# Attention step: scores and minimum of a group's fourth head before the transposes of P's first head, and the output products dealt 5 and 7

## The reference

```python
q = rope(rmsnorm(x @ Wq)); k = rope(rmsnorm(x @ Wk)); v = x @ Wv      # 32 q heads, 8 kv heads of 128
k_all = concatenate([k_cache[block_table], k]); v_all likewise        # 512 cached keys + 128 new
scores = where(valid, q @ k_all.T * SCALE, -1e30)
probs = softmax(scores)                                               # called P here
x = x + (probs @ v_all) @ Wo
```

## Time and profile before

| what | value |
|---|---|
| median of 3 runs | 1405.84 us (1405.07 to 1408.55) |
| the profiled execution | 1408.16 us, its span 1406.0 us |
| busy: TensorE, weight loads | 1392.1 us (99%), 1206.8 us (86%) |
| busy: VectorE, ScalarE, GpSimd | 1094.7 us (78%), 852.8 us (61%), 802.5 us (57%) |
| granted clock of TensorE, mean | 0.998 |

### The profile page before, as it was taken

How to read it: one execution, slowest core, us unless ns; L and a number is a source line. 1 busy time by engine, 2 the same in 40 slices (tenths; PEclk the granted TensorE clock), 3 DMA queues, 4 the chain that set the end, 5 groups by cost and what they waited for, 6 DMA issues and landing times.

```text
span 1406.0 us, 26951 instructions
## 1 busy us (share of the span) xinstructions
PE 1392.1 (99%) x8035; PEld 1206.8 (86%) x8035; DVE 1094.7 (78%) x2220; ACT 852.8 (61%) x2092; POOL 802.5 (57%) x799
## 2 busy tenths in 40 slices
PE   7999999999999999999999999999999999999999
PEld 5888888888888888888888888888888888888887
DVE  7788888888888888888888888888888666654543
ACT  6677666666666666666666666666677423433332
POOL 6555555555555666666666666666566331444442
PEclk9999999999999999999999999999999999999999
DMA  5533333333333222322222223232332540343341
GB/s 179 164 110 110 111 103 104 107 107 104 104 102 105 69 71 65 72 65 65 66 73 67 66 66 74 65 69 49 85 91 65 155 105 24 105 140 106 113 124 69
DMA packets 191440, 129.87 MB, mean 92 GB/s; under 512 B 118832, under 2 KB 158384, under 8 KB 188864
## 3 DMA queue, kind: packets, MB, share of 16 engines
q1 hardware_dynamic: 181808, 110.98, 29.7%
q10 hardware_dynamic: 9072, 16.07, 3.8%
q0 software_dynamic: 416, 1.11, 0.3%
HBM read 125.25 MB, written 24.64 MB: 107 GB/s over the span
## 4 chain that ended last, share of the span: by engine, by line
PE 96%; DMA 1%; DVE 1%; SPq 1%; POOL 1%; issue 0%; ACT 0%; DVEq 0%
PE banks L328 22%; PE banks L329 22%; PE banks L330 22%; PE banks L1456 12%; PE banks L1430 10%; PE banks L1392 2%; PE banks L1400 1%; PE banks L1687 1%; PE banks L1701 1%; PE banks L1514 1%; DMA acc<-in_x 1%; PE banks L1640 1%; PE banks L1408 0%; DMA kv_raw<-in_kv,row_at 0%; SPq L348 0%; PE banks L1539 0%
## 5 line engine op out<-in xcount | busy, mean ns | idle before, releaser
L754 ACT ACTIVATE prob<-prob,nbias 128x640 f32<-128x640 f32 x256 | 210.3, 822 | 145.7 <-DVE nbias L1037 145.7
L1008 DVE TENSOR_TENSOR pt_pair<-banks,pt_pair 128x640 fp32r<-128x640 f32 x256 | 210.8, 824 | 100.8 <-ACT pt_pair L750 98.3
L1037 DVE CUSTOM_DVE_ANT_0 prob<-banks,mask,q_rs 128x640 f32<-128x640 f32 x256 | 220.1, 878 | 39.5 <-PE banks L330 39.5
L1456 PE MATMUL banks<-w_pair,o_pair 128*128 128x512 f32 x768 | 223.6, 413 | 0.0
L750 ACT ACTIVATE pt_pair<-banks 128x640 fp32r<-128x640 f32 x256 | 179.4, 701 | 38.6 <-PE banks L1430 38.6
L1430 PE MATMUL banks<-ident,prob 128*128 128x128 f32 x1280 | 184.2, 274 | 1.2 <-DVE pt_pair L1008 1.1
L1430 PEld LDWEIGHTS banks<-ident,prob 128*128 128x128 f32 x1280 | 146.6, 140 | 43.5 <-issue 31.6
L328 PE MATMUL banks<-w_pair,x_pair 128*128 128x256 f32 (+1 forms) x512 | 179.4, 350 | 3.3 <-DVE acc L1062 3.0
L329 PE MATMUL banks<-w_pair,x_pair 128*128 128x256 f32 (+1 forms) x512 | 174.0, 340 | 0.0
L330 PE MATMUL banks<-w_pair,x_pair 128*128 128x256 f32 (+1 forms) x512 | 173.3, 338 | 0.0
L328 PE MATMUL banks<-kt_pair,qt_pair 128*128 128x320 f32 x512 | 163.6, 320 | 0.7 <-DVE kt_pair L1008 0.7
(11 more groups left out here) (196 smaller groups left out, 3436.3 us busy)
## 6 DMA issues: line engine op xcount, KB each, us to landing
w_raw<-in_w_att SPq DMA_DIRECT2D x56, 320.0 KB, 3.1
w_raw<-in_fw SPq DMA_DIRECT2D x66, 256.0 KB, 3.2
kt_all<-in_kT SPq DMA_DIRECT2D x128, 128.0 KB, 2.5
x_raw<-in_xT ACTq DMA_DIRECT2D x61, 256.0 KB, 2.8
kv_raw<-in_kv SPq DMA_DIRECT2D x384, 32.0 KB, 1.7
kt_raw<-kt_all SPq DMA_DIRECT2D x38, 256.0 KB, 3.0
kv_raw<-in_kv SPq DMA_DIRECT2D x608, 16.0 KB, 1.6
fb_all<-in_gu_b SPq DMA_DIRECT2D x32, 176.0 KB
```

The lines of the kernel that those rows point to most:

```text
L754: act.activation(prob[:, h, :], prob[:, h, :], ACT.Exp, bias=nbias[:, h:h + 1], scale=-1.0, accum_out=psum_row[:, h:h + 1]).then_inc(exped, 1)
L1008: dve.tensor_tensor(pair[1], src, pair[0].bitcast(F32), ALU.subtract).then_inc(lo_sem, 1)
L1037: dve.tensor_tensor_reduce(out=prob[:, h, :].rearrange("p (a n) -> p a n", a=2), in0=score_ps[h % 2][:, :, 0:HALF], in1=mask[:, n % B, :]. ...
L1456: last = pe.matmul(misc_ps, o_pair[:, j, h, :], w_pair[:, k, ds(at + h * HID, HID)], start=i == 0, stop=i == 3 * REP - 1)
```

## The change

In steps 1 to 62 three things move; nothing is added or left out. On TensorE, scores of head 3 go from behind head 0's transposes to before them, so that these stand directly ahead of the transposes of q and of the key. The 12 output products, which stood as 2 before the transposes of head 1, 8 behind them and 2 behind those of head 2, stand as 5 before head 1's and 7 before head 2's. On VectorE, mask_min of head 3 goes ahead of pt_low of head 0. Step 0 is written in another way and keeps its order.

```diff
--- before.py
+++ after.py
@@ -1135,8 +1135,8 @@
                     normalise(n, 2)
                 if not first:
                     o_low(n - 1)
+                    mask_min(n, par, 3)
                     pt_low(n, 0)
-                    mask_min(n, par, 3)
                 qt_low(n + 1)
                 kt_low(n + 1)
                 pt_low(n, 1)
@@ -1473,28 +1473,28 @@
                 if first:
                     scores(n, 2)
                 project_q(n + 1, 1 - par)
-                if not first:
+                if first:
+                    transpose_p(n, 0)
+                    scores(n, 3)
+                    pe.wait_ge(kv_copied, 2)
+                    keep_awake(7, 4)
+                else:
                     scores(n, 2)
                     values(n - 1, 1 - par)
-                transpose_p(n, 0)
-                scores(n, 3)
-                if first:
-                    pe.wait_ge(kv_copied, 2)
-                    keep_awake(7, 4)
+                    scores(n, 3)
+                    transpose_p(n, 0)
                 transpose_q(n + 1)
                 if n + 1 < BY_ROWS:
                     transpose_cached_k(n + 1, 1 - par)
                 transpose_new_k(n + 1, 1 - par)
                 if not first:
-                    project_out(n - 1, 0, 2)
+                    project_out(n - 1, 0, 5)
                 transpose_p(n, 1)
                 if first:
                     keep_awake(7, 4)
                 if not first:
-                    project_out(n - 1, 2, 10)
+                    project_out(n - 1, 5, 12)
                 transpose_p(n, 2)
-                if not first:
-                    project_out(n - 1, 10, 12)
 
             pe.wait_ge(mask_done, 1)
             keep_awake(4, WARM[0])
```

## The result

The changed kernel takes **1440.36 us** (median of 6 runs, 1439.58 to 1444.09), the kernel before 1407.07 us beside it (6 runs). The ratio is **1.0253**, 95% interval 1.0242 to 1.0264: 2.5% slower. The medians are 33.3 us apart; the profiled spans, 1442.0 and 1406.0 us, are 36.0 apart.

A forecast was written before the change was run, and what follows sets the result against it. TensorE, busy 99%, was taken to be held between heads by emptying P's one PSUM tile; a late step's 0 + 0 - 0.32 + 0.90 + 0.11 = +0.69 us, early +0.49, gave +37.5 us: 1443 us, range 1432 to 1456.

The forecast's parts named there:

- The loop: Emptying P's one PSUM tile: 2.46 to 2.48 us between successive heads' first transposes, whatever TensorE does between.
- Rival A: Late loads are a price of changing from products to transposes, not a wait: no change, 1405 us; chance 0.06.
- Rival B: Joined transposes give ScalarE and VectorE time to empty pt_ps, waits before heads 1 and 2 go: 1398 us; chance 0.04.
- Rival D: As forecast, but with the wait for the sum into acc behind head 3 hidden: 1437 us; chance 0.06.
- part 5: Behind head 3's transposes, project_kv waits for VectorE's sum into acc: a new wait of 0.11 us a step.
- Part 1: Scores of head 3 enter the stretch from head 3 to head 0, which grows by 0.87 us in full.
- Part 2: Head 0's transposes join q's and the key's: one join fewer, worth about 0.01 us, taken as nothing.
- Part 3: Output products 5, 7, 0: in late steps head 0 to 1 and 1 to 2 unchanged, 2 to 3 0.32 us less.
- Part 4: VectorE takes head 3's minimum before P's low part of head 0: costs and gains nothing.
- Rival C: P's low part of head 0 on VectorE held up by GpSimd, up to 1.0 us a step: 1504 us; chance 0.04.
- The sum: Total growth with step 1 left out: 23 early steps at 0.49 us and 38 late at 0.69 us, 37.5 us.

The follow-up runs named there:

- the two doses: One extra ScalarE copy ahead of head 2's high part: in the kernel before 1422.70 us, ratio 1.0127; in the changed kernel 1470.52 us, ratio 1.0465.
- the kernel with q's piece: Kernel before with the first three matmuls of q's projection ahead of head 3's transposes, output products 3, 9, 0: 1400.06 us, ratio 0.9966.

## Why the prediction was right

**The loop** was read rightly from one chain of rows. It stood at 2.45 to 2.49 us in every kernel in which the own work between two heads was less and VectorE free, and it moved by 0.49 when ScalarE's part did. Rival A, the price of changing, is refuted by the two doses and by the kernel with q's piece, where the loads are early. Rival B, the faster way, needed a loop under 2.19 us; none was seen. Rival D differs from the forecast only in part 5, and the median, 1440.4, lies almost midway between its 1437 and the 1443 forecast. So the time does not choose between them; the load at 620.81 and the two runs with the sum earlier do, for the forecast. No run gives P a second tile in PSUM, which would test the loop from the other side.

**Part 1** (scores ahead, +0.87 in head 3 to 0): alone it gave 9.90 from 9.03, exactly that.

**Part 2** (the join of transposes, worth about 0.01 us): not tested by itself. In early steps, where head 0 to 1 is own work, 2.67 was forecast and 2.69 measured, so the join brings no gain that shows.

**Part 3** (5, 7, 0 leaves all three stretches on the loop): 2.45, 2.49, 2.48, and 0.32 less from head 2 to 3. Right.

**Part 4** (the swap costs and gains nothing): right for late steps, where the low part started at 614.30, 0.03 behind the end of ScalarE's copy at 614.27. It was too short for early steps: there the swap gains 0.17 us. With it the minimum runs while VectorE would wait for the copy of head 0; without it the minimum stands behind head 0's low part and pushes the long low part of the keys, and so head 1's low part, back. The sum holds, because it was made for the order with the swap; what the swap was worth was not seen.

**Part 5** (a new wait of 0.11 us for the sum into acc): 0.09 to 0.10 measured. The mechanism is right, the size a little large.

**Rival C**, a hold-up of VectorE by GpSimd, did not come. GpSimd in the changed kernel, at head 0's low part:

```profile
613.72 1.57 POOL L521 TENSOR_TENSOR v_pair<-kv_raw,v_pair 128x640 fp32r<-128x640 f32 x1
```

The low part began at 614.30, inside this one, and took 0.83 us.

**The sum**: 37.5 us forecast, 33.3 between the medians, 36.0 between the profiled spans. Within the profiles steps 2 to 24 grew by 11.3 us, as forecast: 0.50 a step for 0.49, and 0.43 to 0.45 in steps 3 to 6. Steps 25 to 61 grew by 25.0 us, 0.66 to 0.69 each for 0.69. The rest is the scores of one step. The scores that are moved stand ahead of head 0 of their own step, so in the last stretch of the step before. Those of step 2 fall into step 1, which grew by 0.05 us only (23.01 and 23.06 us) under the load of x into acc; so the scores of 60 steps cost time and not those of 61. At the other end this shows as step 62, which has none in its last stretch and fell by 0.26 us (14.35 to 14.09 us).

The medians hold something more that no term of the sum has. In the profile before, TensorE waits 2.96 us for the sum of x into acc, and the granted clock is then 0.50 (1.2 GHz) from 56 to 62 us; in the one after it is 0.56 on average there. Both are at 1.00 (2.4 GHz) from 62 us on, and head 0 of step 2 starts at 67.4 and 67.3 us. In the eight profiles whose clock stayed at 1.00 it starts at 61.9 to 64.0 us. So two medians can differ by some 3 us from this alone (an estimate from these starts), which is why small effects are read here from the stretches.

## What to carry to other kernels

Where one buffer is passed round three engines, add up its loop from rows and hold it against the own work of the busy engine in each stretch between two uses; a stretch under the loop waits, however full the engine looks on average. Work is worth most where it fills such a stretch, so grouping like instructions may lose what it was to save. Read lateness off the weight loads, and count only what it moves from start to start.

## What was not expected of the hardware

- TensorE's waits can be almost invisible in its matmul view: in the changed kernel 67.4 us of issue idle at the loads stood against 11.3 us of idle and 1.1 us of named wait at the matmuls, since the recorded end of one matmul lies at or close to the late start of the next (ahead of head 3 at 620.25 for 620.24). With longer waits the matmul rows name VectorE: 31.0 us in the changed kernel with the dose, 42.9 us with the scores alone.
- A product's first start after transposes costs 0.09 us more, but the last of the transposes gives 0.08 of that back (0.03 us to the next start in place of 0.11): 613.80 to 613.83 in the changed kernel. Going back and forth between the two kinds is all but free here.
- The release is very regular: from the end of VectorE's operation to the weight load that waits for it 0.11 to 0.13 us, in every step read of all kernels.
